# Four-stage kernel on one core: the third operand stack later, a part of the causal masks in VectorE's maxima, and the recurrent stage's neighbour with rounded parts

## The reference, cut to what matters

```python
x = x + attention(layernorm(x))   # 16 heads, causal softmax, latent keys and values
x = x + ffn(layernorm(x))         # gated recurrence
x = x + deltanet(layernorm(x))    # 4 heads, chunks of 64 tokens
x = x + ffn(layernorm(x))         # the same weights again

# attention, folded: scores = (q k_eff) c_kv^T / 4, masked, softmax, times c_kv, times v_eff
attn = jnp.where(causal, attn, -jnp.inf); attn = softmax(attn)

# ffn: 64 steps of 64 rows
ft = sigmoid(xt @ wf.T + c @ uf.T + bf); it = sigmoid(xt @ wi.T + c @ ui.T + bi)
gt = tanh(xt @ wc.T + c @ uc.T + bc);    c = ft * c + it * gt
h = tanh(x @ wo.T + c_final @ uo.T + bo)

# deltanet: h = silu(conv of 4 taps); q, k = l2norm(h Wq), l2norm(h Wk); v = h Wv
# beta = sigmoid(h Wb); gate = silu(h Wg); per chunk and head:
A = jnp.tril(kb @ kc.T, -1); U = solve_triangular(eye + A, vc * bc - kb @ S, lower=True)
o = qc @ S + jnp.tril(qc @ kc.T) @ U;  S = S + kc.T @ U
out = rms(o) * norm_w * gate @ Wo
```

## Time and profile before

| | before |
|---|---|
| runs (3) | 1300.27 to 1302.86 us, median 1302.04 us |
| profiled execution | 1304.74 us, its span 1302.8 us |
| mean granted TensorE clock | 0.965 |
| PE, PEld | 1181.0 us (91% of the span), 735.7 us |
| DVE, ACT, POOL | 842.9 us (65%), 667.6 us (51%), 390.3 us (30%) |
| attention, first Ffn, Delta, second Ffn | from 0, 650, 790 and 1137 us on, roughly |

### The profile page before, as it was taken

How to read it: one execution, slowest core, us unless ns; L and a number is a source line. 1 busy time by engine, 2 the same in 40 slices (tenths; PEclk the granted TensorE clock), 3 DMA queues, 4 the chain that set the end, 5 groups by cost and what they waited for, 6 DMA issues and landing times. The chain is left out here.

```text
span 1302.8 us, 32378 instructions
## 1 busy us (share of the span) xinstructions
PE 1181.0 (91%) x13506; PEld 735.7 (56%) x13506; DVE 842.9 (65%) x1815; ACT 667.6 (51%) x1449; POOL 390.3 (30%) x614
## 2 busy tenths in 40 slices
PE   6769999999999999999799997868898777899995
PEld 3334444444444444443578885535676666688884
DVE  6666767776688787782354358698967463465355
ACT  4436666666666666666522236755564223252232
POOL 5420505050400000001353114745464223634210
PEclk9889999999999999998899998988999899999998
DMA  6882445454454444300000000102111210000003
GB/s 206 161 182 49 83 49 98 50 99 51 81 68 50 50 51 50 51 2 1 1 1 1 1 25 11 32 11 56 34 39 18 52 30 15 3 1 1 1 3 126
DMA packets 78753, 61.65 MB, mean 47 GB/s; under 512 B 41360, under 2 KB 65552, under 8 KB 78480
## 3 DMA queue, kind: packets, MB, share of 16 engines
q1 hardware_dynamic: 77456, 57.18, 24.7%
q10 hardware_dynamic: 1152, 2.41, 0.6%
HBM read 38.20 MB, written 20.97 MB: 45 GB/s over the span
## 5 line engine op out<-in xcount | busy, mean ns | idle before, releaser
L727 ACT ACTIVATE weights<-psum 128x512 f32<-128x512 f32 (+1 forms) x608 | 322.7, 583 | 161.9 <-PE psum L628 159.9
L777 DVE TENSOR_REDUCE maxima<-psum 128x1 f32<-128x512 f32 (+3 forms) x432 | 262.5, 664 | 52.4 <-PE psum L550 51.4
L628 PE MATMUL psum<-q_stack,k_stack 99*128 99x512 bf16 (+3 forms) x768 | 224.0, 329 | 0.9 <-ACT weights L727 0.8
L550 PE MATMUL psum<-k_stack,q_stack 96*128 96x512 bf16 (+3 forms) x768 | 212.7, 328 | 2.0 <-DVE maxima L777 2.0
L645 PE MATMUL psum<-weights,v_rows 128*17 128x512 f32 (+3 forms) x1536 | 162.5, 495 | 0.1
L522 POOL TENSOR_TENSOR residual<-residual,att_o 128x256 f32<-128x256 f32 x32 | 23.3, 727 | 357.5 <-DVE att_o L810 357.5
L1012 PE MATMUL psum<-f_xT,f_weights_hi 128*128 128x512 f32 x384 | 123.3, 403 | 4.4 <-DVE f_weights_lo L956 2.3
L1054 ACT ACTIVATE f_gates<-psum,ffn_biases 128x512 f32<-128x512 f32 x72 | 49.6, 690 | 140.2 <-PE psum L1018 132.4
L777 DVE TENSOR_REDUCE negmax<-psum 128x1 f32<-128x384 f32 (+3 forms) x176 | 102.4, 636 | 28.1 <-PE psum L550 26.3
L628 PEld LDWEIGHTS psum<-q_stack,k_stack 99*128 99x128 bf16 x768 | 72.5, 98 | 83.3 <-ACT weights L727 37.9
L1096 DVE TENSOR_TENSOR f_state<-f_gates 128x512 f32<-128x512 f32 x32 | 27.2, 849 | 116.2 <-POOL f_gates L971 73.5
(11 more groups left out here) (164 smaller groups left out, 2196.1 us busy)
## 6 DMA issues: line engine op xcount, KB each, us to landing
qk_parts<-a_parts SPq DMA_DIRECT2D x32, 384.0 KB, 4.3
q_stack<-qk_parts SPq DMA_DIRECT2D x90, 128.0 KB, 7.3
k_stack<-qk_parts SPq DMA_DIRECT2D x90, 128.0 KB, 7.9
residual<-in_x SPq DMA_DIRECT2D x8, 512.0 KB, 7.5
out_x<-residual SPq DMA_DIRECT2D x8, 512.0 KB, 3.0
ffn_weights<-in_ffn_w ACTq DMA_DIRECT2D x1, 2048.0 KB, 9.1
systems<-d_attnT_k_kb_v SPq DMA_DIRECT2D x32, 64.0 KB, 1.8
d_systems<-systems SPq DMA_DIRECT2D x4, 512.0 KB, 3.5
```

The lines of the kernel that those rows point to most:

```text
L550: m = e.matmul(out[:, i * width:(i + 1) * width], self.qst[st][0:self.ROWS, h, qb * P:(qb + 1) * P], self.kst[st][0:self.ROWS, h, k0:k0 + ...
L628: m = e.matmul(out[:, j * width:(j + 1) * width], self.kst[st][0:self.ROWS + self.MAX_ROWS, h, kb * P:(kb + 1) * P], self.qst[st][0:self.R ...
L727: e.activation(self.weights[n % 2][:, heads[0]:heads[-1] + 1, 0:width], bank[self.score_bank[n, i]][:, 0:len(heads) * width].rearrange("p ...
L777: e.tensor_reduce(to, bank[self.bank[item]][:, 0:len(heads) * width].rearrange("p (h x) -> p h x", h=len(heads)), AXIS_X, ALU.max, negate= ...
```

## The change

It moves the third stack's loads behind the later parts; makes the one-head diagonal maxima of attention on DVE with one operation that adds a mask row, takes the minimum of the negated sum and writes the row's result; puts the feed-forward weights' load later, and a second time for the second Ffn, since the store that holds them is used by Delta in between; and gives Delta's projections rounded parts of features and weights, in 6 matmuls instead of 2. It also moves the last sums of the first Ffn and the second group's layernorm within Delta.

```diff
@@ Kernel @@
-        self.mask16 = sb("mask_scores16", [P, P], BF16)
+        self.later16 = sb("mask_scores16", [P, BANK], BF16)
+        self.mask16 = self.later16[:, BANK - P:BANK]
...
+        e.memset(self.later16[:, 0:BANK - P], 0.0).then_inc(*self.s["const16"].did("none"))
@@ Attention @@
-    EARLY = 4
+    EARLY, FFN_LOAD = 4, 100
...
+    def ends_on_diagonal(pair):
+
+        qb, c, width, heads = pair
+        diagonal = c * BANK + width == (qb + 1) * P
+        return diagonal, diagonal and len(heads) == 1
...
-            if item == ("qk", 1, *self.PROJECTED[-1]):
-                for u in range(1, STACKS):
+            for u, g in ((1, 1), (2, 3)):
+                if item == ("qk", g, *self.PROJECTED[-1]):
                     load(u, (0, 1))
...
-                diagonal = k0 + width == (qb + 1) * P
+                diagonal, by_vector = self.ends_on_diagonal(self.pairs[w_at])
+                masked = diagonal and not by_vector
...
-                if diagonal:
+                if masked:
                     e.matmul(out[:, 0:len(heads) * width].rearrange("p (h x) -> p h x", h=len(heads))[:, :, width - P:width],
                              k.ident16[:, :], k.mask16[:, :].rearrange("p (o x) -> p o x", o=1).to_broadcast([P, len(heads), P]),
...
-        k.load_ffn_scalar(e)
         for n, items in enumerate(self.during):
+            if n == self.FFN_LOAD:
+                k.load_ffn_scalar(e, self.ffn_w)
...
+                if self.ends_on_diagonal(self.pairs[w_at])[1]:
+                    for w in unmet(k.s["const16"]("none"), self.unread_free(u, w_at)):
+                        e.wait_ge(*w)
+                    e.tensor_tensor_reduce(self.unread[:, 0:width], scores, k.later16[:, BANK - width:BANK], -1.0, HIGH, ALU.add,
+                                           ALU.min, to).then_inc(*s["max_red"].did(u, w_at))
+                else:
+                    e.tensor_reduce(to, scores.rearrange("p (h x) -> p h x", h=len(heads)), AXIS_X, ALU.max, negate=True
+                                    ).then_inc(*s["max_red"].did(u, w_at))
@@ Ffn.split_scalar @@
+        for w in unmet(k.s["ffn_w_in"](*(["again"] if self.early else [])), *free):
@@ Delta @@
-FIRST_SLOT, LAST_SLOT, END_SLOT, LATE = -5, CHUNKS + LAG_OUT, -3, 9
+FIRST_SLOT, LAST_SLOT, LATE, RELOAD = -5, CHUNKS + LAG_OUT, 9, CHUNKS + 4
+FFN_ENDS = (-2, -1, 3, 4)
...
+    TERMS = ((0, 0, 0), (0, 1, 0), (0, 0, 1), (0, 1, 1), (1, 0, 0), (1, 0, 1))
...
-                for kt in range(KT):
-                    m = e.matmul(qk_bank[:, 0:NQ + DH], cols[kt], self.w_qkb[:, kt, :], start=kt == 0, stop=kt == KT - 1)
+                for i, (v, wp, kt) in enumerate(self.TERMS):
+                    m = e.matmul(qk_bank[:, 0:NQ + DH], cols[v][kt], self.w_qkb[:, wp, kt, :], start=i == 0, stop=i == len(self.TERMS) - 1)
...
-                for kt in range(KT):
-                    m = e.matmul(vg_bank[:, :], cols[kt], self.w_vg[:, kt, :], start=kt == 0, stop=kt == KT - 1)
+                for i, (v, wp, kt) in enumerate(self.TERMS):
+                    m = e.matmul(vg_bank[:, :], cols[v][kt], self.w_vg[:, wp, kt, :], start=i == 0, stop=i == len(self.TERMS) - 1)
@@ Delta.scalar @@
+                e.activation(self.acc[kt][:, :], self.acc[kt][:, :], ACT.Silu).then_inc(*s["features_a"].did("silu", G, kt))
+                e.activation(self.feature(0, G, kt), self.by_chunks(kt), ACT.Copy).then_inc(*s["features_a"].did("hi", G, kt))
...
-                e.activation(self.hT[G % 2][:, kt, :, :, :].rearrange("p c b t -> p b c t"),
-                             self.acc[kt][:, :].rearrange("p (b c t) -> p b c t", b=B, c=TPG), ACT.Silu).then_inc(*s["hT"].did(G, kt))
-            if slot - END_SLOT in range(B):
-                self.guests["scalar_end"](e, unmet, slot - END_SLOT, 1)
+                if not G:
+                    self.ln_scalar(e, unmet, 1)
+            if slot == RELOAD:
+                for w in unmet(s["vg_mm"](CHUNKS - 1)):
+                    e.wait_ge(*w)
+                k.reload_ffn_scalar(e)
+            if slot in FFN_ENDS:
+                self.guests["scalar_end"](e, unmet, FFN_ENDS.index(slot), 1)
@@ Delta.low_part, called by DVE for group 0 and by POOL for the others @@
+        e.tensor_tensor(self.feature(1, G, kt), self.by_chunks(kt), self.feature(0, G, kt), ALU.subtract)
@@ Delta.weights_scalar and weights_vector, called within the first Ffn @@
+        e.activation(self.parts[which][:, 0, :, :], self.raw[which][:, :, :], ACT.Copy).then_inc(*s["features_a"].did("w_hi", which))
+        e.tensor_tensor(self.parts[which][:, 1, :, :], self.raw[which][:, :, :], self.parts[which][:, 0, :, :], ALU.subtract
+                        ).then_inc(*s["features_v"].did("w_lo", which))
...
+        first.guests |= {"weights": {(GROUPS - 4, 0): ("vg", ()), (GROUPS - 1, 0): ("qkb", first.opens()["buffers"])},
+                         "weights_scalar": delta.weights_scalar, "weights_vector": delta.weights_vector}
```

More of the change, by code:

```diff
@@ L405, in stack_free, with unread_free @@
         return self.s["scores"](n, len(self.scored[n]) - 1) if u >= STACKS else None
+    @staticmethod
+    def ends_on_diagonal(pair):
+        qb, c, width, heads = pair
+        diagonal = c * BANK + width == (qb + 1) * P
+        return diagonal, diagonal and len(heads) == 1
+    def unread_free(self, u, w):
+        ahead = [(v, i) for v in range(u + 1) for i, pair in enumerate(self.pairs) if self.ends_on_diagonal(pair)[1] and (v, i) < (u, w)]
+        return self.s["max_red"](*ahead[-1]) if ahead else None
     def diagonal(self, n):
@@ L843, in __init__ @@
     def __init__(self, k, tag, x_ready, before, ahead, early=None):
-        self.k, self.before, self.ahead, self.guests, self.early = k, before, ahead, {}, early
+        self.k, self.before, self.ahead, self.guests, self.early, self.ffn_w = k, before, ahead, {}, early, k.ffn_w
         with ExitStack() as ctx:
@@ L849, in sb @@
                 return ctx.enter_context(k.nc.sbuf_tensor(tag + name, shape, dt))
+            if not early:
+                sb("unused", [P, UNUSED[0]])
             xT = {i: sb(f"xT{i}", [P, 2, KT, BANK], F32R) for i in (0, 2, 1)}
@@ L1145, in vector @@
             keep_state(p, 0)
+            for n in (0, 1):
+                if (p, n) in self.guests.get("weights", {}):
+                    self.guests["weights_vector"](e, unmet, self.guests["weights"][p, n][0])
             renew_state(p, 0)
@@ L1220, in ring @@
                 return [sb(f"{name}{i}", shape) for i in range(n)]
-            self.w_qkb = sb("w_qkb", [P, KT, NQ + DH])
-            self.w_vg = sb("w_vg", [P, KT, 2 * HV])
+            self.hT = [sb("hT0", [P, 2, KT, TPG, B, CH], F32R)]
+            with ExitStack() as early:
+                self.raw = {which: early.enter_context(k.nc.sbuf_tensor("d_raw_" + which, [P, KT, n], F32))
+                            for which, n in (("vg", 2 * HV), ("qkb", NQ + DH))}
+            self.hT.append(sb("hT1", [P, 2, KT, TPG, B, CH], F32R))
+            self.w_vg = sb("w_vg", [P, 2, KT, 2 * HV], F32R)
+            self.w_qkb = sb("w_qkb", [P, 2, KT, NQ + DH], F32R)
             self.conv = sb("conv", [P, KT, 4])
@@ L1389, in gpsimd @@
             G, step = self.front(slot)
[L1390 removed]
+            if G and G > 1 and step == 0:
                 self.ln_gpsimd(e, unmet, G)
             if G is not None and step == 1 and G:
[L1393 removed]
+                for w in unmet(s["xT"](G - 1, KT - 1), *([s["features_v"](G - 2, KT - 1, self.TAPS - 1), s["tap"](G - 2, KT - 1)] if G >= 2 else []),
                                *self.before):
@@ L1428, in gpsimd @@
                 e.tensor_scalar(ss[:, 0:DH], ss[:, 0:DH], EPS, None, ALU.mult).then_inc(*s["q_eps"].did(c))
+            for kt in self.convolved(G, step) if G else ():
+                self.low_part(e, unmet, G, kt)
             Go, left = divmod(slot - LAG_S - TPG, TPG)
@@ L1624, in scalar @@
                              ).then_inc(*s["wu"].did(c))
-            if G and step == 0:
+            if G and G > 1 and step == 0:
                 self.ln_scalar(e, unmet, G)
@@ L1768, in vector @@
                     solve(1)
-            if slot - END_SLOT in range(B):
-                self.guests["vector_end"](e, unmet, slot - END_SLOT)
+            if G == 0:
+                for kt in self.convolved(G, step):
+                    self.low_part(e, unmet, G, kt)
             if slot >= SOLVE and phase == 1 and slot // SOLVE <= CHUNKS // SOLVE:
@@ L1809, in build @@
         k = Kernel(nc, ctx, io)
-        attention = Attention(k)
-        first = Ffn(k, "f1_", attention.updated, attention.ends(), (0, 1))
-        delta = Delta(k, first.updated, first.opens(), first.products_end(), first.ends())
+        with ExitStack() as store:
+            k.weights_store(store, "ffn_weights")
+            attention = Attention(k)
+            first = Ffn(k, "f1_", attention.updated, attention.ends(), (0, 1))
```

(3 more changed lines are left out.)

111 lines of the change are left out of this document (73 added, 38 removed).

## The result

| | before | changed |
|---|---|---|
| median of 11 runs each | 1302.04 us (1299.44 to 1306.38) | 1294.90 us (1291.56 to 1298.99) |
| ratio | | 0.9942, 95% interval 0.9926 to 0.9957 |
| profiled execution, span | 1304.74, 1302.8 us | 1294.09, 1292.1 us |

That is 7.5 us faster (5.6 to 9.6), outside the forecast range of 1261 to 1292. Lines of the changed kernel differ: L820 is L782, L815 and L812 are L777, L1053 is L1012, L1068 is L1027, L1031 is L990, L1551 and L1556 are L1489 and L1494.

A forecast was written before the change was run, and what follows sets the result against it. PE was taken to bound attention's middle, chained waits for stores the prologue, with Delta's middle nearly full on PE. -9.5 - 11 - 7 = -27.5, and 2.7 off to the median, took 1304.7 to 1275 us; range 1261 to 1292.

The forecast's parts named there:

- Third stack: Prologue: loads moved from ahead of the stores close one chained wait of some 9.4 us; -9.5 us, ends -13 and -4.
- the dearer pairs: Attention's one-head maxima on DVE: 0.19 us more per chained pair, 0.07 per unchained; 2 us taken in the prologue.
- Masks off PE: Attention: 240 mask matmuls at 0.058 us leave a full PE, 13.9 us less a fifth; -11 us, ends -14 and -3.
- B: Attention: DVE's pair is dearer, 0.3 to 0.4 us, DVE level with PE; about 1283 us, chance 0.12.
- F: Attention: the DVE operation's main part runs at half rate, making the kernel slower; +50 us, about 1352, chance 0.06.
- Delta, forecast -7: Delta: projections -6, seam -2, added copies and subtractions +1; -7 us, ends -13 and 0.
- -0.5 us per chunk: Delta's projections on PE: six matmuls on rounded parts take 2.27 us per chunk for 2.79 before.
- the term of +1: Delta: the added 16 ACT copies and 14 POOL subtractions cost +1 us, PE waiting at most for one.
- Rival D: Delta gives nothing: silu, copy and POOL's subtraction precede a group's first chunk and slots lengthen; about 1282 us, chance 0.08.
- The seam: Delta's seam: four `normed` on ACT move earlier, two last sums' tanh go to slots 3 and 4; -2 us.
- What was costed at nothing: First Ffn's four splits of delta's weights, feed-forward load at step 100 (no delay), its second issue (0 to +2 us).

The follow-up runs named there:

- stack_alone: The kernel before with only the third stack's loads moved behind the later stores: ratio 0.9936 to before, -8.3 us.
- two_unread: stack_masks with two buffers, taken in turn, for the row that nobody reads: median 1283.38 us, ratio 0.9840 to before.
- hi_twice: Changed kernel making no low features; each projection's last two matmuls read the rounded part again: ratio 0.9853 to before, -19.1 us.
- ends_old: Changed kernel with the first Ffn's ends at slots -3 to 0 as before: ratio 0.9969 to before, -4.0 us.
- stack_masks: The kernel before with only the third stack's late loads and the one-head masks on DVE: median 1286.48 us, ratio 0.9884 to before.

## Why the prediction failed, step by step

- **Third stack, forecast -9.5 (ends -13, -4) with the dearer pairs.** The mechanism held, the size was too high. Alone it gave 8.3 us (5.6 to 11.1), with both edits 3.8 to 7.2 by the profiles, so the 9.5 is 2.3 to 5.7 too much. The three chained waits went as one, and DVE's dearer pairs, counted at 2 us, took at least 1 (`stack_alone` is 8.3 ahead at the second unit's join, both together up to 7.2). The four stores that were issued behind the loads land in 7.7 to 11.0 us, where the four of before took 17.9 to 19.5. The clock was the part that I could not size: it fell in 80 to 90 us instead in five of the twelve profiles.
- **Masks off PE, forecast -11 (ends -14, -3).** Held: -9.2 over the 14 units between the two joins, 0.041 us for each of their 224 masks. The sum had 0.058 less a fifth; it is less three tenths. A late unit fell from 31.05 to 30.52 us between its joins, for a forecast of 30.1 to 30.2; with the second buffer it is 30.26, so most of what was missing is the chained wait. The pair's price was a little off: forecast 0.19 for a chained one; the trace has 0.24. A pair's first instruction is as long as the reduce that it replaces, the accumulator's read starts 0.61 us after it, and the next starts 0.23 us after that:

```profile
459.42 0.69 DVE L812 CUSTOM_DVE_ANT_0 unread<-psum,mask_scores 128x512 bf16<-128x512 f32 x1
460.03 0.08 DVE L812 DVE_READ_ACCUMULATOR2_ANT negmax<- 128x1 f32 x1
460.26 0.69 DVE L812 CUSTOM_DVE_ANT_0 unread<-psum,mask_scores 128x512 bf16<-128x512 f32 x1
```

  Pairs stand 0.84 us apart against 0.60; an unchained one costs nothing, as the next reduce starts with the read. I had put the read at 0.156 by L225 (not quite the shortest of that trace: L1351 has 0.151), and it is 0.083. Rivals B and F fall. The Trainium skill, page "VectorE: DVE Perf Modes", section "The DRAIN you can't avoid", has it that a semaphore between two operations costs nothing extra, measured on copies. For these pairs that is not borne out: from the read's start to the next pair's start it is 0.23 us with the wait and 0 in `two_unread`, without it.
- **Delta, forecast -7 (ends -13, 0).** This is the step that failed; D was +6.5. Its first half, "-0.5 us per chunk", was right on PE, and with no low parts made the whole of Delta gives 5.0 (`hi_twice`, 387.1 for 392.1), where the sum had 8 (6 and 2) ahead of this term. What failed is the term of +1 for what was added: "the matmuls of low features stand last of six, so PE waits at most for one of them, and POOL is at 26.94 of 40: +1". PE indeed does not stand for POOL's part in the changed kernel. But I asked only whether POOL had room and whether PE would wait for its result. I did not ask what DVE does meanwhile, and PE stood 23.1 us for DVE in this stage before the change already. The +1 measured 11.5 us of D, of which 5.7 is that POOL and DVE hold each other up. Rival D had the sign of the missing gain, at a size that was too small.
- **The seam, forecast -2.** With the new features its ends alone were worth 3.5 us of time (`ends_old`), with float32 ones about 1, within the spread.
- **What was costed at nothing** stayed so: the first Ffn is as long as before, its groups 17.2 us earlier from first to last.

The sum of what held is -15.1 us (`stack_masks`), where the forecast had -20.5; the difference to the result lies in Delta.

The trace of before had shown the effect, in a row that I had not read. In the feed-forward stages the `tensor_tensor` L1096 of DVE, with two SBUF inputs, runs beside POOL's `tensor_tensor` L971 in 5 of its 32 executions and takes 1.69 to 1.71 us there, and 0.69 in the others:

```profile
652.61 2.54 POOL L971 TENSOR_TENSOR f_gates<-f_gates 128x512 f32<-128x512 f32 x2
```

```profile
654.00 1.69 DVE L1096 TENSOR_TENSOR f_state<-f_gates 128x512 f32<-128x512 f32 x1 [7.63 <-POOL f_gates L971]
...
681.72 0.69 DVE L1096 TENSOR_TENSOR f_state<-f_gates 128x512 f32<-128x512 f32 x1 [5.05 <-issue]
```

It would have priced the step: 14 holds of up to 1.0 us, on a DVE that is busy for 34.5 of 37 us from 851 to 888 us, with the first solves.

## What to carry to other kernels

An engine's idle share does not say that work put on it is free. For a GpSimd operation that reads SBUF, list the VectorE instructions with two SBUF inputs that will run beside it, and add up to the length of the GpSimd operation for each; a look for instructions of VectorE that are longer than their kind in the trace at hand prices it. And before a part of work is taken off an engine, read in the same stage what the chain runs through: in the middle of attention 224 masks of 58 ns gave 9.2 of 13 us, in Delta taking out a third pair of matmuls, twice in each of 32 chunks, gave nothing that could be measured, as PE then stood for DVE instead.

## What the runs showed that I had not expected

- A GpSimd subtraction of 1.28 us holds a VectorE `tensor_tensor` or `scalar_tensor_tensor` with two SBUF inputs until 0.1 to 0.3 us after its own end (0.55 for one of 512 columns); a memset of the same tile (0.52 us) holds none. A copy, which reads one tensor and takes 0.61 us, holds too. Cutting the subtraction in two frees DVE of a third of its excess (8.9 to 6.0 us) and lengthens POOL's part to 1.41 to 1.9 us for the pair, and the kernel is slower by 3.5 us.
- The read of the accumulator behind a maximum of 512 columns is 83 ns long and costs nothing unless the next operation waits for it, then 0.23 us.
